# Mixture-of-experts block loop: the second weights are split once ahead of the loop instead of once per block

## The reference

```python
def _L0_ffn_ref(x, w1, b1, w2, b2, centroids, w_route):
    ...
    logits = cos_scores + route_scores
    gates = _top_k_softmax(logits, TOP_K)
    h = jax.nn.gelu(jnp.einsum('bsd,edh->bseh', x, w1) + b1, approximate=False)
    expert_out = jnp.einsum('bseh,ehd->bsed', h, w2) + b2
    out = jnp.einsum('bse,bsed->bsd', gates, expert_out)
    return out
x = x + jnp.tanh(g_xattn[0]) * _L0_xattn_ref(ctx_2048, _layernorm(x, axis=-1), L0_xattn_b, itok_Bx1_68_817)
x = x + jnp.tanh(g_ffn[0]) * _L0_ffn_ref(_layernorm(x, axis=-1), ...)
```

## Time and profile before

| | us |
|---|---|
| median of 3 runs | 2145.31 |
| lowest, highest | 2139.34, 2153.35 |
| the profiled execution | 2141.61 |
| its span, first to last instruction | 2139.6 |
| TensorE busy | 1901.1 (89%) |
| VectorE busy | 1597.0 (75%) |
| ScalarE busy | 1127.1 (53%) |
| GpSimd busy | 737.5 (34%) |

### The profile page before, as it was taken

One profiled execution on the slowest core, in us unless ns is written; L12 is line 12 of the kernel. 1 busy time (PEld: TensorE's weight loads), 2 busy tenths in 40 slices (PEclk: granted clock), 3 DMA queues, 4 the chain that ended last, 5 costly groups with the idle time before them and its releaser, 6 DMA issues. The chain is left out here.

```text
span 2139.6 us, 38585 instructions
## 1 busy us (share of the span) xinstructions
PE 1901.1 (89%) x10720; PEld 1060.5 (50%) x10721; DVE 1597.0 (75%) x3742; ACT 1127.1 (53%) x1999; POOL 737.5 (34%) x547
## 2 busy tenths in 40 slices
PE   0599999999999999999999999998399988989887
PEld 0344444444444444444444444443277766767675
DVE  6578788777877878877777787773477777777776
ACT  0166655656556565655655665654155555555554
POOL 1112111111111111211201111100168888888887
PEclk9899999999999999998999999998599999999999
DMA  3878687676867877777777786653358677777674
GB/s 110 141 109 162 117 181 139 133 153 125 179 133 137 178 142 134 162 114 173 142 130 151 126 184 111 140 125 125 98 114 145 135 132 138 149 125 131 131 135 67
DMA packets 173114, 292.01 MB, mean 136 GB/s; under 512 B 37982, under 2 KB 42078, under 8 KB 172944
## 3 DMA queue, kind: packets, MB, share of 16 engines
q1 hardware_dynamic: 140016, 222.26, 51.0%
q0 software_dynamic: 32928, 67.68, 17.8%
HBM read 127.09 MB, written 71.63 MB: 93 GB/s over the span
## 5 line engine op out<-in xcount | busy, mean ns | idle before, releaser
L918 DVE TENSOR_REDUCE mx<-bank 128x1 f32<-128x512 f32 x1024 | 693.8, 687 | 243.6 <-PE bank L714 231.5
L622 ACT ACTIVATE prob<-bank 128x512 f32<-128x512 f32 x1024 | 579.6, 596 | 492.1 <-PE bank L702 491.4
L590 POOL TENSOR_TENSOR regrouped_then_w<-regrouped_then_w 128x512 fp32r<-128x512 f32 x128 | 166.5, 1301 | 1145.9 <-ACT regrouped_then_w L612 1145.9
L714 PE MATMUL bank<-stA,stB 98*128 98x512 f32 x1024 | 428.4, 420 | 67.4 <-DVE mx L918 40.8
L702 PE MATMUL bank<-stB,stA 100*128 100x512 f32 x1024 | 469.2, 460 | 9.8 <-issue 9.5
L702 PEld LDWEIGHTS bank<-stB,stA 100*128 100x128 f32 x1024 | 196.9, 193 | 212.5 <-ACT prob L622 116.3
L675 PE MATMUL bank<-prob,vin 128*32 128x512 f32 x2048 | 279.6, 619 | 0.0
L675 PE MATMUL bank<-prob,ones 128*32 128x512 f32 x2048 | 278.9, 617 | 0.0
L1150 POOL DMA_INDIRECT rows_in<-xn_rows,gather_ids x152 | 221.3, 1456 | 162.7 <-DVE rows_in L1360 121.3
L714 PEld LDWEIGHTS bank<-stA,stB 98*128 98x128 f32 x1024 | 202.8, 198 | 113.2 <-DVE mx L918 73.0
L1180 POOL DMA_INDIRECT out_dram<-yout,scatter_ids x144 | 231.7, 1609 | 39.2 <-issue 30.4
(11 more groups left out here) (182 smaller groups left out, 2095.6 us busy)
## 6 DMA issues: line engine op xcount, KB each, us to landing
stB<-regrouped_then_w SPq DMA_DIRECT2D x192, 256.0 KB, 5.5
stA<-regrouped_then_w SPq DMA_DIRECT2D x192, 256.0 KB, 8.4
x_k_then_w<-in_x_dram SPq DMA_DIRECT2D x16, 1024.0 KB, 6.1
x_k_then_w<-in_ctx_dram SPq DMA_DIRECT2D x16, 1024.0 KB, 8.6
vin<-in_ctx_dram SPq DMA_DIRECT2D x16, 1024.0 KB, 6.4
xres<-in_x_dram SPq DMA_DIRECT2D x16, 1024.0 KB, 12.8
xn_rows<-xn SPq DMA_DIRECT2D x64, 256.0 KB, 2.2
out_dram<-xres SPq DMA_DIRECT2D x16, 1024.0 KB, 10.5
```

The lines of the kernel that those rows point to most:

```text
L590: pool.tensor_tensor(turnedL[:, side, :], turned[:, side, :], turnedH[:, side, :].bitcast(F32), ALU.subtract).then_inc(s_lo, 1)
L622: act.activation(prob[:, u % 2, j, :], psS[j % 2][:, :], ACT.Exp).then_inc(s_exp, 1)
L714: pe.matmul(psM[s % 2][:, :], stB[0:98, g, j, i * P:(i + 1) * P], stA[0:98, g, j, :], start=True, stop=True).then_inc(s_m, 1)
L918: dve.tensor_reduce(mx[:, s // 4, s % 4:s % 4 + 1], psM[s % 2][:, :], AX.X, ALU.max).then_inc(s_mx, 1)
```

## The change

The split of the second weights is taken out of the step. Ahead of the loop ScalarE copies w2_all of each of the eight experts into a new tile w2_hi (128 partitions x 8192 floats, where w2_parts had 2048), and VectorE subtracts it from w2_all in place, so that w2_all then holds the low parts. The wait of ScalarE for `weights_loaded` moves ahead of these copies. `second` gets the expert of the block before, read by TensorE into a register, and addresses w2_hi and w2_all with it. It waits for all eight subtractions (`w2_lo_parts`), a constant. `weights_hi` and `weights_lo` are now counted once per block.

```diff
-            w2p = sb("w2_parts", [P, 2, KE, D], F32R)
+            w2h = sb("w2_hi", [P, E, KE, D], F32R)
+            w2l = w2_all.bitcast(F32R)
...
-                    def second(st, m):
+                    def second(st, m, expert):
                         pe.wait_ge(f_hs, st.front(2 * KE, -1, 2 * m + 2))
                         if m == 0:
-                            pe.wait_ge(f_wlo, st.front(2, -1, 2))
+                            pe.wait_ge(f_2lo, E)
+                        part = lambda q: (w2h, w2l)[q][:, bass.ds(expert, 1), m, :].rearrange("p a n -> p (a n)")
...
                         if not st.first:
-                            second(st, 0)
+                            back = expert_of(pe, st, -1)
+                            second(st, 0, back)
...
-                        pe.wait_ge(f_wlo, st.front(2, 0, 1))
+                        pe.wait_ge(f_wlo, st.front(1, 0, 1))
...
-                        if st.first:
-                            act.wait_ge(s_w, 16 * 2 * E)
-                        else:
+                        if not st.first:
                             act.wait_ge(f_h, st.front(KE, 0, 0))
...
-                        act.activation(w2p[:, 0, :, :], weights_of(w2_all, expert), ACT.Copy).then_inc(f_whi, 1)
...
+                    act.wait_ge(s_w, 16 * 2 * E)
+                    for e in range(E):
+                        act.activation(w2h[:, e, :, :], w2_all[:, e, :, :], ACT.Copy).then_inc(f_2hi, 1)
                     rounds(act, step)
...
-                        dve.wait_ge(f_whi, st.front(2, 0, 2))
-                        dve.tensor_tensor(w2p[:, 1, :, :], weights_of(w2_all, expert), w2p[:, 0, :, :].bitcast(F32), ALU.subtract).then_inc(f_wlo, 1)
...
                     for i in range(2):
                         dve.memset(rows[:, i, :, :], 0.0).then_inc(f_clear, 1)
+                    for e in range(E):
+                        dve.wait_ge(f_2hi, e + 1)
+                        dve.tensor_tensor(w2l[:, e, :, :], w2_all[:, e, :, :], w2h[:, e, :, :].bitcast(F32), ALU.subtract).then_inc(f_2lo, 1)
                     rounds(dve, step)
```

More of the change, by code:

```diff
@@ L1060, in flamingo_kernel @@
             f_wlo = sem("weights_lo")
+            f_2hi = sem("w2_hi_parts")
+            f_2lo = sem("w2_lo_parts")
             f_xt = sem("rows_turned")
@@ L1223, in second @@
                             last = split_product(pe, psY[c][:, :], lambda p: hT[:, p, m, c * P:(c + 1) * P],
-                                                 lambda p: w2p[:, p, m, :], m == 0, m == KE - 1)
+                                                 part, m == 0, m == KE - 1)
                             if m == KE - 1:
@@ L1236, in step @@
                         if not st.first:
-                            second(st, 1)
+                            second(st, 1, back)
                         rank(st.steps(USES, 0, 2 + USE[KD]), bank_of(st, USE[KD]), expert_of(pe, st, 2), st.steps(1, 2, 1))
-                        pe.wait_ge(f_wlo, st.front(2, 0, 1))
+                        pe.wait_ge(f_wlo, st.front(1, 0, 1))
                         for m in range(KE):
```

2 lines of the change are left out of this document (1 added, 1 removed).

## The result

| | before | after |
|---|---|---|
| median of the runs timed together, us | 2142.69 (2139.34 to 2153.35, 4 runs) | 2120.65 (2119.11 to 2121.86, 4 runs) |
| profiled execution: time / span, us | 2141.61 / 2139.6 | 2121.86 / 2119.7 |
| mean granted clock | 0.955 | 0.965 |

The ratio is 0.989, with a 95% interval of 0.9853 to 0.9928. It comes out 1 us under the first rival ("the loop keeps its mix", 2122 to 2130). Whether the rival's reasons were right is another question, and most of this document is about that.

What follows compares the result with a forecast made beforehand. GpSimd's queue was taken to bound the expert blocks. Against the profiled 2141.6 us, + 8 ahead of the loop - 10 in it = - 2 gave 2139.6; against the median of 2145.3, 2143 (range 2123 to 2160).

Steps and rivals of the forecast that it cites:

- the first rival: In the block loop: short cycles stay, giving 22.9 us back; 2130 or 2122 us in all; chance 0.22.
- What bounds the loop: In the expert blocks GpSimd's queue sets the pace, 516 of 558 us; VectorE's subtraction L1342 costs it time.
- The third rival: Gathers aren't stalled by this kind of VectorE instruction, L1342 only coincides; no change, 2145 us; chance 0.1.
- Part 1: Block loop: without ScalarE's copy and VectorE's subtraction GpSimd gains 0.74 us x 24 + 0.46 us x 11 = 22.9 us.
- what would show it: Signs in the changed trace: third gathers 1.0 us, hold always 0.2 us, first transposes near 1552 instead of 1544.68.
- Part 2: Block loop: TensorE's pause shrinks from about 2 to 1.2 us; gain 6 if all cycles long, 22.9 if mix stays; taken 10.
- Part 5: TensorE's expert-number load ahead of the second product: hidden in the wait for gelu parts; bounds 0 and 10 us, taken 0.
- Part 4: Ahead of the loop: eight VectorE subtractions hold off GpSimd's first gathers; loss from 0 to 9.3 us, taken 8.
- the middle bound: Ahead of the loop: GpSimd gets in between every two subtractions, four gathers each about 0.8 us longer; loss 3 us.
- Part 3: Ahead of the loop: ScalarE's eight copies, 8.4 us, hidden wholly; VectorE's eight subtractions, 9.3 us, alone cost at most 1 us.

## Why the prediction was wrong, step by step

**What bounds the loop: right.** GpSimd's queue, with gathers held off by VectorE instructions that have two SBUF inputs. yout from PSUM removed the 2.65 us gather, and with it 30 us of the kernel after and 41 us of the kernel before. The third rival ("no coupling", 2145) is out. The Trainium skill infers (SBUF — State Buffer, section on who interferes with whom) that a tensor_tensor does not stall descriptor generation. An indirect gather it does stall here: with L1342 gone the third gather fell from 1.73 to 1.00 us, with yout's input moved to PSUM the second from 2.65 to 1.0. Whether it is the writing of descriptors that stands still, or the gather's reading of its indices from SBUF, as the prediction allowed, no run separates.

**Part 1, the 0.74 and 0.46 us: right in kind and nearly in size.** Third gathers of 1.0 us and a hold of 0.2 us came as written under "what would show it". Long cycles gained 0.65 and short ones 0.36. (The part's own terms, 0.74 x 24 + 0.46 x 11, give 22.8 and not 22.9.)

**Part 2, the clock and the pause: right, but for the link between clock and short cycles.** The pause shrank to 0.9 to 1.85 us and the falls of the clock went from 11 cycles to 3 (none with the load moved away). The prediction took the falls for the one cause of short cycles, by way of yout instructions that come one by one. They are one cause of a late second product and not the only one, and what is late behind it is the turned parts: 9 of 12 short cycles came without a fall. Of itself the shorter pause would have made every cycle long, and where it stands alone (moved load, or no split at all) it did. The all-long loop measured 15.63 us a cycle, a gain of 11 us; the prediction had 6 for that case and took 10. The case was sized a little short: 15.78 came from a mean over long cycles with short ones between them, and why such a row of long ones runs at 15.63 was not looked into.

**Part 5, TensorE's load of the expert's number: the step that failed.** It was taken as 0, hidden in the wait for the gelu parts. It isn't hidden: 0.4 to 0.95 us of idle time stand in front of 17 of the 35 second products (4 before), and the product's median start moved from 3.47 to 4.30 us behind the hold. The bounds were 0 and 10 us of loss; measured is a gain of 10 us, by the mean cycles of 15.63 without the load in that place and 15.35 with it. It needs the rest of the change: the load alone in the kernel before gained nothing. The part's last sentence said that being late there "would even push cycles toward the short kind", and then nothing was added to the sum for it. The rival "the mix kept" named this cause as well ("or TensorE's register work delays the second product") and priced it at 22.9 us against a measured 21.1. That the sum is so near is in part luck: the all-long loop gave 11 of it and the load 10, not the 22.9 of an unchanged mix. The rival got 0.22, since the shrunken pause spoke against short cycles of the first kind and short cycles of the second kind were not weighed.

**Part 4, ahead of the loop: the mechanism right, the size wrong.** 8 us were taken, 3.2 measured. The value was chosen by the train of four yout instructions, which shuts GpSimd out altogether. Eight subtractions let GpSimd in between; that was the middle bound, priced at 3. Both trains look alike in the timeline of VectorE, so the nearest row was the wrong guide; the row of L1342, an instruction of the same kind and shape with a gather beside it, would have given 0.73 us for each of the four, that is the 3.

**Part 3, the copies on ScalarE: right.** They ran from 1522.65 to 1530.33, before anybody wanted ScalarE.

The two errors point the same way: 8 - 3.2 = 5 us too much loss ahead of the loop, 21 - 10 = 11 us too little gain in it, and 2 us of luck in the attention part make up the 18 us between the profiled 2121.9 and the 2139.6 of the sum.

## What to carry to other kernels

When an instruction queue on GpSimd is the limit, look at what VectorE runs beside its long instructions, and give such VectorE instructions one input from PSUM before anything else is tuned; here that was worth more than the change itself. Price a new register load on an engine as time in front of the next instruction even where a wait seems to cover it, and ask in which direction a delay acts: in this loop, whose cycles have two kinds, a delay of some 0.8 us off the binding queue changed the count of each kind and gained time. Follow such a delay to what it makes late first; here it was the turned parts and not the gated rows. When a test of a cause comes out empty, look in its trace whether the supposed sign and the effect still go together. And judge an edit by the counts per cycle in the trace, not by the median, when the part of the kernel that it doesn't touch wanders by 10 us.

## What was not expected of the hardware

- A delay on TensorE makes the loop of the changed kernel faster: no load in front of the second product 15.63 us a cycle, one load 15.35, two loads 15.19.
- After pauses of 0.9 to 1.85 us TensorE kept 2.4 GHz in all 26 cases of the kernel with the load moved and all 26 of the one without the split. In the kernel after it kept it in 12 of 15; behind three pauses of 1.40 to 1.45 us, each with another 0.46 to 0.64 us of idle time between transposes and product, the second product ran at 1.2 GHz, and behind others as long it didn't. In the kernel before 17 pauses were longer (1.87 to 2.14 us), and 11 second products ran at 1.2 GHz.
- Four yout instructions without a gap hold a gather off to the end (2.65 to 2.97 us) where VectorE has not paused since its subtraction of the first weights, and let gathers of 1.0 to 1.6 us pass where it has; eight subtractions without a gap (9.10 us for eight) let gathers through at 1.7 to 2.0 us each. With one input of yout in PSUM a gather at the same place takes 1.0 us. What makes the difference is open.
- In the kernel before, the load alone changed nothing (11 short cycles with and without it). Why it needs the rest of the change to make short cycles is open too.
